# Second attention of a fused six-layer kernel: three score banks for the maxima, three for the exponentials, one exponential a bank, first and second scores issued in pairs

## The reference, cut to what matters

```python
qkv = (x @ w_qkv).reshape(B, L, 3, H, D).transpose(2, 0, 3, 1, 4)   # H = 16 heads, D = 8
q = _apply_rope(q, cos, sin)
k = _apply_rope(k, cos, sin)
attn = jnp.einsum('bhqd,bhkd->bhqk', q, k) * scale
attn = jax.nn.softmax(attn, axis=-1)
out = jnp.einsum('bhqk,bhkd->bhqd', attn, v)
return out @ w_proj + b_proj
```

## Time and profile before

| | |
|---|---|
| three runs | 2479.38, 2481.73, 2483.67 us; median 2481.73 |
| the profiled execution | 2477.91 us, of which 2476.0 are the span from the first to the last instruction |
| mean granted TensorE clock | 0.939 of full speed |
| PE busy over the span | 2236.7 us (90%) |
| DVE busy | 1986.3 us (80%) |
| ACT busy | 1298.4 us (52%) |
| first maximum to last maximum of the second attention | 1126.6 to 2043.4 us |
| one tile of it (from one output transpose, line 2081, to that of the next tile) | 57.1 us |

### The profile page before, as it was taken

One profiled execution on the slowest core, in us unless ns is written; L12 is line 12 of the kernel. 1 busy time (PEld: TensorE's weight loads), 2 busy tenths in 40 slices (PEclk: granted clock), 3 DMA queues, 4 the chain that ended last, 5 costly groups with the idle time before them and its releaser, 6 DMA issues.

```text
span 2476.0 us, 33777 instructions
## 1 busy us (share of the span) xinstructions
PE 2236.7 (90%) x11138; PEld 1544.6 (62%) x11138; DVE 1986.3 (80%) x4646; ACT 1298.4 (52%) x1907; POOL 1024.6 (41%) x953
## 2 busy tenths in 40 slices
PE   4499588779599999977999999999999999999999
PEld 3377366557377777764555555555555556777777
DVE  6588588768488888867888888888888886888887
ACT  1088333278444444433666666666666665444444
POOL 6646445536545655552211122212222203555554
PEclk9999666589789999996999999999999999999999
DMA  7243211144188887852222222222222206787887
GB/s 184 80 156 125 41 35 39 44 154 150 49 188 173 175 183 162 183 125 56 79 72 69 71 65 69 68 65 70 68 76 71 80 29 138 163 186 168 183 182 155
DMA packets 146489, 274.14 MB, mean 111 GB/s; under 512 B 21055, under 2 KB 24138, under 8 KB 146070
## 3 DMA queue, kind: packets, MB, share of 16 engines
q1 hardware_dynamic: 129942, 242.61, 41.1%
q0 software_dynamic: 16384, 29.46, 5.6%
HBM read 212.92 MB, written 54.65 MB: 108 GB/s over the span
## 4 chain that ended last, share of the span: by engine, by line
PE 40%; DVE 7%; DMA 5%; ACT 2%; issue 2%; SPq 0%; POOL 0%; DVEq 0%; ACTq 0%
PE ps L2029 12%; PE ps L2053 10%; PE ps L2040 9%; DMA gate_rows<-gates_dram 4%; DVE m L1429 2%; PE ps L1750 2%; DVE shift L1594 2%; PE ps L1752 2%; PE ps L1751 2%; PE ps L2062 1%; ACT hi L869 1%; PE ps L2095 1%; DMA gates_dram<-gateT 1%; DVE gate L1384 1%; PE ps L1764 1%
## 5 line engine op out<-in xcount | busy, mean ns | idle before, releaser
L1594 DVE TENSOR_REDUCE shift<-ps 128x1 fp32r<-128x512 f32 x1024 | 665.8, 685 | 132.9 <-PE ps L2029 127.2
L1019 ACT ACTIVATE prob<-ps 128x1024 f32<-128x1024 f32 x512 | 511.2, 1024 | 309.1 <-PE ps L2040 303.1
L869 ACT ACTIVATE hi<-m 128x512 fp32r<-128x512 f32 x512 | 319.0, 631 | 427.1 <-DVE m L1429 427.0
L707 POOL TENSOR_TENSOR lo<-m,hi 128x512 fp32r<-128x512 f32 x256 | 349.1, 1368 | 389.0 <-ACT hi L869 388.9
L2029 PE MATMUL ps<-k_pad,q_st 128*128 128x512 f32 x1024 | 405.2, 438 | 14.6 <-DVE shift L1594 7.2
L1429 DVE SCALAR_TENSOR_TENSOR m<-ps,gate_rows 128x512 f32<-128x512 f32 x512 | 334.8, 680 | 91.4 <-PE ps L1752 52.7
L2029 PEld LDWEIGHTS ps<-k_pad,q_st 128*128 128x128 f32 x1024 | 180.7, 190 | 271.1 <-DVE shift L1594 190.9
L2040 PE MATMUL ps<-q_sh,k_pad 128*128 128x512 f32 x1024 | 330.2, 404 | 0.0
L2053 PE MATMUL ps<-prob,v_cols 128*32 128x512 f32 x2048 | 272.7, 605 | 0.4 <-ACT prob L1019 0.4
L1096 DVE TENSOR_TENSOR lo<-m,hi 128x512 fp32r<-128x512 f32 x256 | 220.4, 861 | 16.8
L1750 PE MATMUL ps<-hi,vals_hl 128*128 128x512 f32 x512 | 211.1, 412 | 5.2 <-DVE lo L1096 4.5
(11 more groups left out here) (215 smaller groups left out, 3847.9 us busy)
## 6 DMA issues: line engine op xcount, KB each, us to landing
gate_rows<-gates_dram SPq DMA_DIRECT2D x254, 512.0 KB, 12.0
w_blk<-w_dram SPq DMA_DIRECT2D x38, 514.5 KB, 3.7
q_st<-q_dram SPq DMA_DIRECT2D x64, 256.0 KB, 2.7
k_pad<-k_dram SPq DMA_DIRECT2D x256, 50.0 KB
k_dram<-qk_hl SPq DMA_DIRECT2D x48, 256.0 KB, 4.9
q_dram<-qk_hl SPq DMA_DIRECT2D x48, 256.0 KB, 3.0
x_blk<-sorted_x SPq DMA_DIRECT2D x38, 258.0 KB, 3.7
rope<-rope POOLq DMA_DIRECT2D x64, 128.0 KB, 3.3
```

The costliest lines, as they stand in the source:

```text
L707: pool.tensor_tensor(m["lo"][:, s], m["m32"][:, s], m["hi"][:, s].bitcast(F32), ALU.subtract).then_inc(sig(ph, "lo_pool"), 1)
L869: return act.activation(o, i, ACT.Copy)
L1019: act.activation(prob[:, h % HP, 2 * half:2 * half + 2, :], ps[:, b0:b0 + 2, :], ACT.Exp, scale=SCALE).then_inc(sig(ph, "prob"), 1)
L1594: dve.tensor_reduce(shift[:, g % 2, b, c:c + 1], wide(PASS1 + b % 2), AXX, ALU.max, negate=True).then_inc(sig(ph, "qmax"), 1)
```

## The change

The eight banks are dealt anew: banks 0 to 2 for the first scores, 3 to 5 for the second (before: 0 and 1, and 2 to 5). Both kinds go around their three banks, so the n-th matmul of a kind waits for the reader of the matmul three before it. The exponentials become four instructions of 128x512 a step instead of two of 128x1024, each with a semaphore count of its own. PE's step is reordered: second scores 0 and 1; early work; first scores 2 and 3 of head h + 5; `values` of step h - 1; second scores 2 and 3; first scores 0 and 1 of head h + 6; late work. The orders on ACT, DVE, POOL and SP stay as they are, except that each half of the exponentials is now two instructions, and that the counts in SP's waits are doubled.

```diff
-        PASS1, PASS2, OB, MISC = 0, 2, 6, 7
+        PASS1, PASS2, OB, MISC = 0, 3, 6, 7
...
-                    pass_wait(sp, sig(4, "st"), t * 2 * HEADS - 2 * HEADS + 8 * g + 8)
+                    pass_wait(sp, sig(4, "st"), t * 4 * HEADS - 4 * HEADS + 16 * g + 16)
...
-            sp.wait_ge(sig(4, "st"), (TILES - 1) * 2 * HEADS + HEADS)
+            sp.wait_ge(sig(4, "st"), (TILES - 1) * 4 * HEADS + 2 * HEADS)
...
                 def exps(t, h, half):
-                    act.wait_ge(sig(ph, "st"), t * 2 * HEADS + 2 * h + half + 1)
-                    b0 = PASS2 + 2 * half
-                    act.activation(prob[:, h % HP, 2 * half:2 * half + 2, :], ps[:, b0:b0 + 2, :], ACT.Exp,
-                                   scale=SCALE).then_inc(sig(ph, "prob"), 1)
+                    for j in (2 * half, 2 * half + 1):
+                        n = t * 4 * HEADS + 4 * h + j
+                        act.wait_ge(sig(ph, "st"), n + 1)
+                        act.activation(prob[:, h % HP, j, :], wide(PASS2 + n % 3), ACT.Exp,
+                                       scale=SCALE).then_inc(sig(ph, "prob"), 1)
...
                 def maxima(t, g, j, blocks=range(BLK)):
                     for b in blocks:
-                        dve.wait_ge(sig(ph, "s1"), (t * GROUPS + g) * 16 + 4 * j + b + 1)
+                        n = (t * GROUPS + g) * 16 + 4 * j + b
+                        dve.wait_ge(sig(ph, "s1"), n + 1)
...
-                        dve.tensor_reduce(shift[:, g % 2, b, c:c + 1], wide(PASS1 + b % 2), AXX,
+                        dve.tensor_reduce(shift[:, g % 2, b, c:c + 1], wide(PASS1 + n % 3), AXX,
...
-                        if not (isinstance(t, int) and t == g == 0 and 4 * j + b < 2):
-                            pe.wait_ge(sig(ph, "qmax"), (t * GROUPS + g) * 16 + 4 * j + b - 1)
-                        pe.matmul(wide(PASS1 + b % 2), q_st[:, g % 2, b * P:b * P + P], k_pad[:, HPG * g + j],
+                        n = (t * GROUPS + g) * 16 + 4 * j + b
+                        if n >= 3:
+                            pe.wait_ge(sig(ph, "qmax"), n - 2)
+                        pe.matmul(wide(PASS1 + n % 3), q_st[:, g % 2, b * P:b * P + P], k_pad[:, HPG * g + j],
...
-                def pass2(t, h, half, first=False):
+                def pass2(t, h, heads):
...
-                    if not first:
-                        pe.wait_ge(sig(ph, "prob"), t * 2 * HEADS + 2 * h - 1 + half)
-                    for j in (2 * half, 2 * half + 1):
-                        last = pe.matmul(wide(PASS2 + j), k_pad[:, HPG * g + j, kb * P:kb * P + P],
-                                         q_sh[:, g % 2], start=True, stop=True)
-                    last.then_inc(sig(ph, "st"), 1)
+                    for j in heads:
+                        n = t * 4 * HEADS + 4 * h + j
+                        if n >= 3:
+                            pe.wait_ge(sig(ph, "prob"), n - 2)
+                        pe.matmul(wide(PASS2 + n % 3), k_pad[:, HPG * g + j, kb * P:kb * P + P],
+                                  q_sh[:, g % 2], start=True, stop=True).then_inc(sig(ph, "st"), 1)
...
-                    pe.wait_ge(sig(ph, "prob"), t * 2 * HEADS + 2 * h + 2)
+                    pe.wait_ge(sig(ph, "prob"), t * 4 * HEADS + 4 * h + 4)
...
-                    pass2(t, h, 0, first)
+                    pass2(t, h, (0, 1))
                     early_work(t, p, h, more, before)
                     if scores:
-                        pass1(t1, g, j, (2,))
-                    pass2(t, h, 1, first)
-                    if scores:
-                        pass1(t1, g, j, (3,))
+                        pass1(t1, g, j, (2, 3))
                     if h > 0:
                         values(t, h - 1, p)
                     elif before is not None:
                         values(before, HEADS - 1, 1 - p)
+                    pass2(t, h, (2, 3))
                     pass1_ahead(t, h + 1, more)
                     late_work(t, p, h, more, before)
```

More of the change, by code:

```diff
@@ L2026, in pass1 @@
                     for b in blocks:
-                        if not (isinstance(t, int) and t == g == 0 and 4 * j + b < 2):
-                            pe.wait_ge(sig(ph, "qmax"), (t * GROUPS + g) * 16 + 4 * j + b - 1)
-                        pe.matmul(wide(PASS1 + b % 2), q_st[:, g % 2, b * P:b * P + P], k_pad[:, HPG * g + j],
+                        n = (t * GROUPS + g) * 16 + 4 * j + b
+                        if n >= 3:
+                            pe.wait_ge(sig(ph, "qmax"), n - 2)
+                        pe.matmul(wide(PASS1 + n % 3), q_st[:, g % 2, b * P:b * P + P], k_pad[:, HPG * g + j],
                                   start=True, stop=True).then_inc(sig(ph, "s1"), 1)
-                def pass2(t, h, half, first=False):
+                def pass2(t, h, heads):
                     g, kb = h // HPG, h % HPG
-                    if kb == 0 and half == 0:
+                    if kb == 0 and heads[0] == 0:
                         pe.wait_ge(sig(ph, "qsh_sb"), t * GROUPS + g + 1)
-                    if not first:
-                        pe.wait_ge(sig(ph, "prob"), t * 2 * HEADS + 2 * h - 1 + half)
-                    for j in (2 * half, 2 * half + 1):
-                        last = pe.matmul(wide(PASS2 + j), k_pad[:, HPG * g + j, kb * P:kb * P + P],
-                                         q_sh[:, g % 2], start=True, stop=True)
-                    last.then_inc(sig(ph, "st"), 1)
+                    for j in heads:
[4 more added lines that the diff above has]
+                                  q_sh[:, g % 2], start=True, stop=True).then_inc(sig(ph, "st"), 1)
                 def values(t, h, p):
                     g, kb = h // HPG, h % HPG
-                    pe.wait_ge(sig(ph, "prob"), t * 2 * HEADS + 2 * h + 2)
+                    pe.wait_ge(sig(ph, "prob"), t * 4 * HEADS + 4 * h + 4)
                     if kb == 0 and not (isinstance(t, int) and t == g == 0):
@@ L2160, in step @@
                 def step(t, p, h, more, before=None):
-                    first = h == 0 and before is None
                     ahead = h + AHEAD
```

## The result

The changed kernel takes 2494.97 us in the median of 8 runs (2491.04 to 2501.21), the kernel before 2483.68 us (2479.38 to 2488.39, 8 runs). The ratio is 1.005, with a 95% interval of 1.0034 to 1.0065: slower, by 8 to 16 us. The forecast was 2494 us, and slower.

The account below looks back on a forecast made before the run. PE's own instructions were taken to set the pace, with 0.77 us of bank waits a tile. +1.06 us a tile gave +15.9 and the ends -3.8, total +12.1: 2494 us, range 2481 to 2511.

Parts of the forecast that it names:

- What bounds the kernel: Second attention: PE's own instructions set the pace; waits for banks in steps 5 and 6 cost 0.77 of 57.1 us a tile.
- The gain: Steps 5 and 6: the new deal of banks takes away at most the 0.77 us of waiting a tile.
- the third bank's own delay: Steps 5 and 6: a head's last first score still waits for its first maximum, 0.1 us each, 0.2 a tile.
- 0.13 for `o_raw`: Step 5: `values`, first of its group, waits for ACT's copy `o_raw` until 1.14 instead of 1.01, 0.13 us.
- The tie that costs: Step 7: second score 3 waits for exponential 0, which stands behind the second rope copy: 1.40 us plus 0.10 for restart.
- The sum: One tile: -0.77 + 0.2 + 0.13 + 1.50 = +1.06 us; over 15 tiles with rope copies, +15.9.
- The ends: Ahead of the first step, first and last tile, and last steps: -3.0, -2 and +1.2, together -3.8 us.
- bare steps: Steps of 3.03 us without the early or late work; those of the first and last tile were to give -2 us.
- The last steps: Steps without first scores: `values` waits for the last exponential, +0.1 for four steps and about +0.7 more, +1.2 us.
- Thin margins in many steps: Rival, chance 0.13: second score 1 misses its 0.06 us margin in seven steps without late work, +16 us, so 2510.
- Faster, if the transfer lands sooner: Rival, chance 0.10: rope transfer under 4.8 us instead of 6.28, no stall in step 7, -10.4 us, so 2471.
- No change, with a transfer of about 5.5: Rival, chance 0.12: rope transfer takes about 5.5 us, the stall 0.7 with its restart, sum 0, so 2482.

Follow-up runs that it names:

- e2: Changed kernel with both transfers of part 1 issued on POOL ahead of `rope_low` of part 0, a semaphore for each part: 2466.19 us, 0.9968 of the kernel before.
- e1: Changed kernel with the second rope copy on ACT moved from the head of step 7 to that of step 8: 2467.55 us, 0.9981 of the kernel before.
- e8: Changed kernel with the second rope copy on ACT moved to the head of step 6: ratio 1.0414 to the kernel before.

## Why the prediction was right

*What bounds the kernel.* I named PE's own instructions, with 0.77 us of waits in steps 5 and 6. Steps 5 and 6 were indeed the only ones that gained more than 0.03 us.

*The gain.* I had 0.77 less 0.2 for the third bank's own delay and 0.13 for `o_raw`. Steps 5 and 6 gave back 0.39 together, against 0.44. The rows show the parts: second scores 0.25 apart instead of 0.23, first scores 0.33 apart (the 0.1 for the maximum of block 0), and 0.73 from there to `values` in step 5 where 0.65 is asked in step 6. The last two were in the sum.

*The tie that costs.* Its chain came out link by link, from the start of step 5 at 1521.61: first rope copy at 0.95 (taken 0.98), transfers at 2.91 (3.07), second copy at 9.04 (9.35), score 3 released at 10.20 (10.53). The stall is 1.33 us in the median with its restart; I had 1.50. The first link, that ACT reaches the first copy 0.9 us later than before because exponentials of step 4 now stand ahead of it, is in these numbers (0.95 where it was 0.07), and e2 shows the last: without the transfer's lateness, no stall.

*The sum.* A tile cost 1.03 us more, forecast 1.06: the gain came out 0.05 smaller and the stall 0.17 smaller, and the other 13 steps together cost 0.1 that I did not have. All 15 tiles with a rope copy have the stall, also the first (step 7: 4.85 us, after 3.50). Times 15 that is 15.5, forecast 15.9.

The ends gave -3.4, forecast -3.8. The first second score came 2.94 us sooner after the value projection (28.00 to 25.06), forecast 3.0. DVE there:

```profile
1139.53 4.87 DVE L1596 TENSOR_REDUCE shift<-ps 128x1 fp32r<-128x512 f32 x8 [2.60 <-PE ps L2032]
```

eight maxima in 4.87 us, 0.60 apart, where pairs took 1.58. The first and the last tile, forecast 2 for their bare steps, gave 2.9: the first took 56.68 us after 57.65, 2.0 less than a tile of +1.03 would, and the last tile's steps 0 to 10 took 0.9 less. But only half of that is bare steps. Steps 8, 9 and 10 of the first tile gave 0.6; 1.45 came from its step 0 (5.63 to 4.18), of which 4.6 us ran at the lower level of the clock before and 2.0 after; in e1 and e2, where it was 4.5 and 4.3, the step took 5.19 and 5.10. So some 0.9 of it is when the clock rises.

The last steps cost 2.4, forecast 1.2, and that is the term that was mis-sized most. The steps without first scores take 2.67 (2.51 in the earlier trace rows), as worked out:

```profile
2069.64 0.73 PE L2044 MATMUL ps<-q_sh,k_pad 128*128 128x512 f32 x2
...
2072.31 0.73 PE L2044 MATMUL ps<-q_sh,k_pad 128*128 128x512 f32 x2
```

Not in the sum was that the `values` in step 13, the first of its group, now waits for the copy `o_raw`, which ACT starts at 2073.81, behind the last two exponentials of step 12 (step 13: 2.50 to 3.25):

```profile
2074.56 1.06 PE L2056 MATMUL ps<-prob,v_cols 128*32 128x512 f32 x8 [0.57 <-ACT o_raw L869]
```

From the start of step 15 to the last transpose it cost 1.0, forecast 0.7. So the total of 12.1, which is the forecast's own 12.1, rests on a mechanism that came out and on errors of 0.4 to 1.2 us that cancel. That they cancel to the last 0.1 is luck, and so are the 0.9 us of the clock.

*The rivals.* Thin margins in many steps: not seen, steps 2, 4, 10, 14 and 15 are within 0.03 us of before. Faster, if the transfer lands sooner: false for this kernel (it took 6.36 us on average from issue to copy, 6.28 before), but e2 made it true, and shows that the condition was rightly named. No change, with a transfer of about 5.5: false by the same 6.36. With the stall gone the kernel gains 0.2 to 0.3%, where the faster rival's -10.4 us is 0.4%. In e2 the stage is 6.4 us shorter: a tile is 0.30 shorter where the rival had 0.44, and the ends give the rest of the miss.

## What to carry to other kernels

When a buffer is taken from one ring and given to another, look not at average slack but at each instruction that can be late on the releasing engine: here a copy that waits for a transfer, in one step of sixteen, hidden for as long as a bank could stay full for a whole step. Ask for every wait that costs nothing today what hides it, and move the late work (a transfer's issue, or the copy that waits for it) before the cover is taken away; the same change was then a gain of 0.2 to 0.3%. Compare stages within profiles and totals by ratio on one chip: here the spans of two profiles differed by 21.6 us, of which 12.1 were the change.

## What the runs showed of the hardware

Of two transfers of 128 KB in a row the second took a median of 5.8 us from issue to landing where three stores of 256 KB were issued 0.14 us behind the first, and 2.9 where the stores came 3.1 us behind it (the first transfer took 4.2 and 2.6). And idle stretches of PE of 4.3 to 4.9 us (e8) cost more than themselves: the granted clock was between 0.50 and 0.68 of full speed over the next 5 us, and step 7 took 1.9 us more in the median of 14 tiles. The idle stretch of about 1 us in step 7 of the changed kernel left the clock at 1.00.
